# Causal mask of the row maxima: mask products on TensorE replaced by an add-and-max on VectorE

## The chip, the cores and the metric

One core of a Trainium2 chip runs the whole program. The metric is device time of the kernel in microseconds, the median of several runs. Lower is better. The five engines of a core (TensorE for matmul, VectorE, ScalarE, GpSimd, SyncE) each run their own instruction stream in program order and meet only at semaphores.

## What is computed

For each of 16 batches of 512 tokens with 256 features, a gated block of attention and a feed-forward net:

```python
xn = layernorm(x)
q, k, v = proj(Wq), proj(Wk), proj(Wv)          # 16 heads of 16
scores = einsum('bhsd,bhtd->bhst', q, k)
scores = where(triu(ones((S, S)), k=1), -inf, scores)
attn = softmax(scores / sqrt(D))
s = einsum('bhst,bhtd->bhsd', attn, v) @ Wo.T
g = silu((silu(xn @ wg.T) * (xn @ wu.T)) @ wd.T)   # wg, wu, wd: integers / 127
out = x + s * g
```

All is fp32. The kernel reaches fp32 accuracy by splitting most operands into a high and a low part (fp32r).

## The kernel before

The work of one batch is cut into units, each with a two-letter name and an index. Three hand-written tables (`HEAD`, `PERIOD`, `TAIL`) give the one order in which all engines walk through the units. `PERIOD` is run 13 times, and one pass of it is one batch's worth of work, with units of three neighbouring batches mixed (the second number of a unit says how many batches ahead it belongs). A unit function such as `u_sm` is called once for each engine, and emits that engine's part.

The units that matter here:

- `sm` (lines 419 to 437): scores of queries by keys, needed only for the maximum of each row. There are 22 such units in a batch, listed in `MAXIMA` (line 35). Query block `i` (0 to 3) needs the keys 0 to 128(i+1). A unit fills two banks of PSUM (one bank for the even head of each pair and one for the odd head) with as many pairs of heads as fit: 4 pairs at i=0 (2 x 4 x 128 columns), 2 at i=1 (2 x 2 x 256), 1 at i=2 (2 x 384) and 1 at i=3 (2 x 512). Over a batch that is 2 units with i=0, 4 with i=1, 8 with i=2, and 8 with i=3.
- `mk` (lines 439 to 457): TensorE adds the causal mask to the diagonal block of those scores by four small bf16 products a unit, and signals `f_sm`. VectorE waits for `f_sm`, takes the maxima of both banks in one `tensor_reduce` into `row_max`, and signals `d_sm`.
- `mt` transposes the maxima. Negated, they go by DMA into spare rows of `q_stack`, so that the products of the `st` units give score minus maximum, keys by queries. ScalarE takes their exponential, GpSimd zeroes what is above the diagonal, and `pv` multiplies by v.
- `gg`, `gu`, `hs`, `dn` are the feed-forward net. VectorE takes part in each (lines 366, 379, 416). `la` are the layer norm's statistics (lines 225 to 233).

PSUM has seven banks for all this (`RING`) and an eighth for `pv`. The last numbers of a unit in a table are its banks. Before TensorE writes a bank, `prev` waits for the release of the bank's last user; for `sm` that is `d_sm`, VectorE's maximum (line 42). A piece of `PERIOD` (lines 92 and 93):

```python
v 2 0 2, sm 2 6 34, mk 2 6 34, st 1 14 01, sm 2 7 56,
mk 2 7 56, pv 1 6, sm 2 8 34, mk 2 8 34, st 1 15 12, xr 1 0, sm 2 9 56
```

So `sm 8` on banks 3 and 4 can't start before the maximum of unit 6 on the same banks is taken.

At the start, GpSimd fills constants (lines 738 to 769), the mask's two factors `PICK` and `MASK` among them, and only then begins its part of the units, whose first is the power in line 237.

Of the kernel before, what the change touches and what calls it, by code (L numbers as in the profile page):

```python
# [4 lines left out]
FP32, F32R, BF16, INT32 = mybir.dt.float32, mybir.dt.float32r, mybir.dt.bfloat16, mybir.dt.int32  # L5
ACT = mybir.ActivationFunctionType
ALU = mybir.AluOpType
AX = mybir.AxisListType

P = 128  # L10
B, S, E = 16, 512, 256
# [5 lines left out]
TT = S // P  # L17
PAIRS = H // 2
HALF = 2 * P
STACK = 64  # L20
# [3 lines left out]
SCALE_S = 1.0 / D ** 0.5  # L24
EPS = 1e-5
MASKED = -3.0e38

COUNT = dict(
    f_gm=3, d_gm=3, f_tr=2, d_xm=1, f_qk=4, f_v=2, f_gg=FT, f_gu=FT, f_dn=2, f_op=2, f_mt=2, f_sm=22, f_st=20, f_pv=12,
# [79 lines left out]
def build(nc, x, xT, wqT, wkT, wvT, woT, wgT, wuT, wdT, out, scratch_o, scratch_r, scratch_m):  # L109
    with ExitStack() as ctx:  # L110
        def sb(name, shape, dt=FP32):
            return ctx.enter_context(nc.sbuf_tensor(name, shape, dt))

        def sem(name):
            return ctx.enter_context(nc.semaphore(name))
# [14 lines left out]
        QS = [sb(f"q_stack{i}", [P, PAIRS, S]) for i in range(2)]  # L130
        KS = [sb(f"k_stack{i}", [P, PAIRS, S]) for i in range(2)]
        V = [sb(f"v{i}", [P, TT, H, VW]) for i in range(2)]
        MX = sb("row_max", [P, 2, P])
# [16 lines left out]
        PICK = sb("mask_rows_bf16", [P, 2, P], BF16)  # L150
        MASK = sb("causal_mask", [P, 4, 64], BF16)
        ZERO = sb("zeros", [P, 512], BF16)

        PS = ctx.enter_context(nc.psum_tensor("bank", [P, RING, 512], FP32))
        PVB = ctx.enter_context(nc.psum_tensor("values", [P, 512], FP32))
# [1 line left out]
        sems = {name: sem(name) for name in COUNT}  # L157
        s_flag, s_lowrow, s_half = sem("s_flag"), sem("s_lowrow"), sem("s_half")
        s_first = [sem(f"s_first{t}") for t in range(TT)]
        s_const, s_fixed = sem("s_const"), sem("s_fixed")  # L160
        s_zeros, s_ones, s_kfill, s_qfill = sem("s_zeros"), sem("s_ones"), sem("s_kfill"), sem("s_qfill")
        s_w = {w: sem(f"s_w{w}") for w in W}
        c_wf, c_wh, c_wl = sem("c_wf"), sem("c_wh"), sem("c_wl")
# [6 lines left out]
        def r(ap):  # L170
            return ap.bitcast(F32R)

        def both(banks):
            return PS[:, banks[0]:banks[1] + 1:banks[1] - banks[0], :]
# [5 lines left out]
        def wait(e, s, value):  # L180

            if value > 0:
                e.wait_ge(s, value)

        def after(e, name, beta, k):
            wait(e, sems[name], nth(name, beta, k))

        def signal(ins, name):
            ins.then_inc(sems[name], 1)
# [229 lines left out]
        def u_sm(en, e, beta, par, k, banks, prev):  # L419
            i, pairs = MAXIMA[k]  # L420
            keys, half = P * (i + 1), k // (len(MAXIMA) // 2)
            if en == "pe":
                if k % (len(MAXIMA) // 2) == 0:
                    for which in range(2):
                        wait(e, s_stack[2 * half + which], 48 * (beta + 1))
                    if half == 0 and beta == 1:
                        e.wait_ge(s_rows, 32)
                    elif half == 0 and beta > 1:
                        wait(e, s_zero, 16 * (beta - 1))
                prev(e)  # L430
                for j, pair in enumerate(pairs):
                    for parity, n in enumerate(banks):
                        low = 64 * parity
                        nc.tensor.matmul(PS[:, n, j * keys:(j + 1) * keys],  # L434
                                         r(QS[par][low:low + STACK, pair, i * P:(i + 1) * P]),
                                         r(KS[par][low:low + STACK, pair, 0:keys]), start=j == 0, stop=False,
                                         skip_group_check=True)

        def u_mk(en, e, beta, par, k, banks, prev):
            i, pairs = MAXIMA[k]  # L440
            keys, n, half = P * (i + 1), len(pairs), k // (len(MAXIMA) // 2)
            if en == "pe":
                for right in range(2):
                    for parity, m in enumerate(banks):
                        low = 64 * parity
                        scores = PS[:, m, 0:n * keys].rearrange("p (n t) -> p n t", n=n)
                        last = nc.tensor.matmul(scores[:, :, i * P + 64 * right:i * P + 64 * right + 64], PICK[low:low + 64, right, :],  # L447
                                                MASK[low:low + 64, 0:n, :], start=False, stop=right == 1, skip_group_check=True)
                signal(last, "f_sm")
            elif en == "dve":  # L450
                after(e, "f_sm", beta, k)
                if beta == 0:
                    e.wait_ge(s_const, 19)
                at = pairs[0] % (PAIRS // 2)
                rows = MX[:, half, 32 * half:32 * half + 32].rearrange("p (b n i) -> p b n i", b=2, i=TT)[:, :, at:at + n, i]
                scores = both(banks)[:, :, 0:n * keys].rearrange("p b (n t) -> p b n t", n=n)
                signal(e.tensor_reduce(rows, scores, axis=AX.X, op=ALU.max), "d_sm")  # L457
# [189 lines left out]
        def u_rw(en, e, beta, par, k, banks, prev):  # L647
            if en == "sp":
# [4 lines left out]
                e.dma_start(QS[1][MROW:P:4, :, :].rearrange("p a (i s) -> p (a i) s", i=2),  # L653
                            ZERO[0:32, :].bitcast(FP32).rearrange("p (o s) -> p o s", o=1).to_broadcast([32, 2 * PAIRS, 256]))\
                 .then_inc(s_rows, 16)
# [62 lines left out]
        def run(en, e):  # L718
            users = {}
            step(en, e, 0, HEAD[:BRANCH], users)  # L720
            if en != "pe":
                later_steps(en, e, users)
                return

            e.wait_ge(s_flag, 3)
            exact = e.value_load(FLAG[0:1, 0:1], min_val=0, max_val=1)
            with e.If(exact):
                short[0] = True
                later_steps(en, e, dict(users))
            with e.Else():  # L730
                short[0] = False
                later_steps(en, e, dict(users))
# [3 lines left out]
        @block.gpsimd  # L736
        def _(e):
            e.memset(ZERO[:], 0.0).then_inc(s_zeros, 1)
            e.memset(RDEN[:], 1.0).then_inc(s_ones, 1)
            e.memset(IDF[:], 0.0).then_inc(s_const, 1)  # L740
            e.memset(PICK[:], 0.0).then_inc(s_const, 1)
            e.memset(MASK[:], 0.0).then_inc(s_const, 1)
            e.memset(MINUS_HALF[:], -0.5).then_inc(s_const, 1)
            e.wait_ge(s_const, 4)
            e.affine_select(out=IDF[:], in_=IDF[:], compare_op=ALU.not_equal, fill=1.0, base=0,
                            pattern=[[-1, P]], channel_multiplier=1).then_inc(s_const, 1)
            for low in (0, 64):
                e.wait_ge(s_const, 5 + low // 64 * 3)
                for side in range(2):
                    rows = PICK[:, side, 64 * side:64 * side + 63]  # L750
                    e.affine_select(out=rows, in_=rows, compare_op=ALU.not_equal, fill=1.0, base=-low,
                                    pattern=[[-1, 63]], channel_multiplier=1).then_inc(s_const, 1)
                all_masked = PICK[:, 1, 0:64]
                e.affine_select(out=all_masked, in_=all_masked, compare_op=ALU.not_equal, fill=1.0, base=-low - 63,
                                pattern=[[0, 64]], channel_multiplier=1).then_inc(s_const, 1)
            e.affine_select(out=MASK[:], in_=MASK[:], compare_op=ALU.is_ge, fill=MASKED, base=-64,
                            pattern=[[0, 4], [-1, 64]], channel_multiplier=1).then_inc(s_const, 1)
            e.wait_ge(s_const, 12)
            e.memset(MASK[0:64], 0.0).then_inc(s_const, 1)
            e.wait_ge(s_const, 13)  # L760
            e.affine_select(out=MASK[0:64], in_=MASK[0:64], compare_op=ALU.is_ge, fill=MASKED, base=0,
                            pattern=[[0, 4], [-1, 64]], channel_multiplier=1).then_inc(s_const, 1)
            for row in (63, 127):
                e.wait_ge(s_const, 14 + row // 127)
                e.affine_select(out=MASK[:], in_=MASK[:], compare_op=ALU.not_equal, fill=MASKED, base=-row,
                                pattern=[[0, 4], [0, 64]], channel_multiplier=1).then_inc(s_const, 1)
            for v in V:
                e.memset(v[:], 1.0).then_inc(s_const, 1)
            e.memset(MX[:], 0.0).then_inc(s_const, 1)
            run("pool", e)  # L770

        @block.sync
# [12 lines left out]
        def _(e):  # L785
            half = PAIRS // 2
            e.wait_ge(s_zeros, 1)
            zeros = ZERO[:].bitcast(FP32).rearrange("p (o s) -> p o s", o=1).to_broadcast([P, PAIRS, 256])
            for m in range(2):
# [14 lines left out]
        def _(e):  # L804
            e.wait_ge(s_const, 16)
            e.wait_ge(s_zeros, 1)
            nc.tensor.matmul(PVB[:], ZERO[:, 0:P], ZERO[:], start=True, stop=True).then_inc(s_fixed, 1)
            run("pe", e)
# [28 lines left out]
```

## Time and profile before

| what | us |
|---|---|
| median of 3 runs | 947.63 (947.14 to 948.02) |
| span of the profiled execution | 945.8 |
| TensorE busy in it | 914.8 |
| VectorE busy in it | 707.2 |
| ScalarE, GpSimd busy in it | 585.8, 495.1 |

The profiled execution has no total time of its own beyond its span, which runs from the first to the last instruction. The span lies 1.8 us under the median. Matmuls overlap in the pipeline, so a sum of their durations, and the busy time of TensorE, say little of what one of them costs. The chain of work that ended last, and the distances between starts, say it better. An engine that waits shows as idle time before an instruction, with the instruction that released it.

### The profile page before, as it was taken

How to read it: one execution, taken by the hardware profiler on the slowest of the kernel's cores; microseconds unless marked ns; L12 is line 12 of the kernel's file. 1: busy time of each engine (PE TensorE's matmuls, PEld its weight loads, DVE VectorE, ACT ScalarE, POOL GpSimd, SP SyncE). 2: the span in 40 equal slices, each digit the busy share in tenths (PEclk: the TensorE clock that was granted, in tenths of full speed). 3: DMA queues.
4: the chain of work that ended last, by engine and by line, in shares of the span. 5: the costliest groups of instructions: out<-in, count | busy, mean ns of one | idle time of the engine just before them, and what ended most of it. 6: DMA issues, size and time to landing. Idle time of an engine off the chain costs nothing.

```text
span 945.8 us, 22760 instructions
## 1 busy us (share of the span) xinstructions
PE 914.8 (97%) x9065; PEld 685.6 (72%) x9065; DVE 707.2 (75%) x950; ACT 585.8 (62%) x796; POOL 495.1 (52%) x681
## 2 busy tenths in 40 slices
PE   3999999999999999999999999999999999999995
PEld 2777767776868777686877868777786867768654
DVE  5985868778696887868788786877778697776823
ACT  5356664757576675756657575665757557575771
POOL 4253553736456464645636455473745547364553
PEclk9999999999999999999999999999999999999999
DMA  6704235353353534535343453534345253543323
GB/s 221 213 25 170 84 116 169 100 198 132 134 164 127 170 106 179 154 125 171 129 151 126 170 152 117 176 132 158 130 148 162 104 185 120 175 131 135 118 93 98
DMA packets 84507, 133.97 MB, mean 142 GB/s; under 512 B 13680, under 2 KB 34928, under 8 KB 84336
## 3 DMA queue, kind: packets, MB, share of 16 engines
q1 hardware_dynamic: 84400, 132.47, 41.8%
q8 instruction: 75, 1.23, 0.5%
q14 instruction: 32, 0.26, 0.1%
HBM read 53.22 MB, written 25.75 MB: 83 GB/s over the span
## 4 chain that ended last, share of the span: by engine, by line
PE 91%; DVE 2%; DMA 2%; POOL 2%; issue 1%; ACT 1%; SPq 0%; POOLq 0%; ACTq 0%; DVEq 0%
PE bank L194 48%; PE values L525 15%; PE bank L434 12%; PE bank L492 11%; PE bank L447 4%; DMA o_reciprocals<-scratch_r 1%; ACT probs L500 1%; DVE row_max L457 1%; PE bank L463 1%; POOL o_compact L566 1%; PE bank L668 0%; DMA scratch_r<-sum_reciprocals 0%; DVE x_in L259 0%; DVE xt_lo L279 0%; DMA sums<-scratch_o 0%
## 5 line engine op out<-in xcount | busy, mean ns | idle before, releaser
L457 DVE TENSOR_REDUCE row_max<-bank 128x2 f32<-128x768 f32 (+3 forms) x352 | 384.9, 1124 | 63.5 <-PE bank L447 60.3
L500 ACT ACTIVATE probs<-bank 128x1024 f32<-128x1024 f32 x320 | 320.4, 1026 | 122.2 <-PE bank L492 120.8
L507 POOL TENSOR_SCALAR_AFFINE_SELECT probs<-probs 128x256 f32<-128x256 f32 (+1 forms) x448 | 194.0, 450 | 275.1 <-ACT probs L500 274.1
L525 PE MATMUL values<-probs,v 128*17 128x512 f32 (+3 forms) x2048 | 166.2, 436 | 0.9 <-POOL probs L507 0.9
L393 POOL TENSOR_TENSOR h_lo<-gated,h_hi 128x512 fp32r<-128x512 f32 x96 | 124.6, 1298 | 74.8 <-ACT h_hi L390 72.7
L434 PE MATMUL bank<-k_stack,q_stack 64*128 64x128 f32 (+3 forms) x1024 | 155.3, 363 | 1.5 <-DVE row_max L457 1.2
L492 PE MATMUL bank<-q_stack,k_stack 64*128 64x512 f32 (+3 forms) x1024 | 142.2, 350 | 1.3 <-DVE row_max L457 0.7
L434 PEld LDWEIGHTS bank<-k_stack,q_stack 64*128 64x128 f32 x1024 | 83.1, 186 | 66.9 <-issue 30.4
L492 PEld LDWEIGHTS bank<-q_stack,k_stack 64*128 64x128 f32 x1024 | 82.9, 186 | 39.1 <-issue 17.3
L366 DVE SCALAR_TENSOR_TENSOR gated<-gated,bank 128x512 f32<-128x512 f32 x96 | 65.8, 685 | 55.4 <-ACT gated L363 55.4
L194 PE MATMUL bank<-xt_hi,wg_hi 128*128 128x256 f32 x384 | 99.3, 293 | 1.6 <-DVE gated L379 1.6
L194 PE MATMUL bank<-wd_hi,h_hi 128*128 128x256 f32 x384 | 93.7, 284 | 3.3 <-POOL h_lo L393 3.3
L194 PE MATMUL bank<-xt_hi,wu_hi 128*128 128x256 f32 x384 | 96.0, 286 | 0.0
L194 PE MATMUL bank<-xt_lo,wg_hi 128*128 128x256 f32 x384 | 94.0, 279 | 0.0
L194 PE MATMUL bank<-xt_lo,wu_hi 128*128 128x256 f32 x384 | 93.2, 279 | 0.0
L194 PE MATMUL bank<-wd_hi,h_lo 128*128 128x256 f32 x384 | 93.0, 282 | 0.0
L447 PE MATMUL bank<-causal_mask,mask_rows_bf 64*128 64x64 bf16 (+2 forms) x1408 | 84.6, 207 | 0.6 <-issue 0.6
L308 ACT ACTIVATE qk_hi<-bank 128x512 fp32r<-128x512 f32 x64 | 38.3, 598 | 74.6 <-PE bank L194 71.1
L525 PEld LDWEIGHTS values<-probs,v 128*17 128x17 f32 x2048 | 44.6, 96 | 47.6 <-issue 39.8
L194 PEld LDWEIGHTS bank<-xt_hi,wg_hi 128*128 128x128 f32 x384 | 73.3, 191 | 6.6 <-DVE gated L379 1.8
L194 PEld LDWEIGHTS bank<-wd_hi,h_hi 128*128 128x128 f32 x384 | 73.2, 191 | 4.5 <-POOL h_lo L393 3.5
L363 ACT ACTIVATE gated<-bank 128x512 f32<-128x512 f32 x96 | 57.6, 600 | 28.9 <-PE bank L194 28.4
(123 smaller groups left out, 1624.4 us busy)
## 6 DMA issues: line engine op xcount, KB each, us to landing
k_stack<-qk_hi SPq DMA_DIRECT2D x64, 256.0 KB, 2.5
q_stack<-qk_hi SPq DMA_DIRECT2D x64, 256.0 KB, 2.5
scratch_o<-o SPq DMA_DIRECT2D x64, 256.0 KB, 2.2
x_again<-x SPq DMA_DIRECT2D x16, 512.0 KB, 4.7
k_stack<-qk_lo SPq DMA_DIRECT2D x32, 256.0 KB, 2.5
q_stack<-qk_lo SPq DMA_DIRECT2D x32, 256.0 KB, 2.6
o_compact<-scratch_o SPq DMA_DIRECT2D x32, 256.0 KB
o_reciprocals<-scratch_r SPq DMA_DIRECT2D x32, 256.0 KB
```

Source lines behind the costliest of these rows:

```text
L194: last = nc.tensor.matmul(dst, r(lhs[a]), r(rhs[b]), start=start and j == 0, stop=stop and j == len(parts) - 1)
L308: signal(e.activation(r(QKP[0][:, k % 2, :]), PS[:, banks[0], :], ACT.Copy), "d_qh")
L363: signal(e.activation(T[:, slot, :], PS[:, banks[0], :], ACT.Tanh, scale=0.5 * SCALE_W), "d_t")
L366: signal(e.scalar_tensor_tensor(out=T[:, slot, :], in0=T[:, slot, :], scalar=1.0, in1=PS[:, banks[0], :], op0=ALU.add, op1=ALU.mult), "d_a")
L393: signal(e.tensor_tensor(r(HT[1][:, f:f + 2, :]).rearrange("p f s -> p (f s)"), T[:, slot, :], HT[0][:, f:f + 2, :].rearrange("p f s -> p ...
L434: nc.tensor.matmul(PS[:, n, j * keys:(j + 1) * keys], r(QS[par][low:low + STACK, pair, i * P:(i + 1) * P]), r(KS[par][low:low + STACK, pai ...
L447: last = nc.tensor.matmul(scores[:, :, i * P + 64 * right:i * P + 64 * right + 64], PICK[low:low + 64, right, :], MASK[low:low + 64, 0:n, ...
L457: signal(e.tensor_reduce(rows, scores, axis=AX.X, op=ALU.max), "d_sm")
L492: last = nc.tensor.matmul(PS[:, n, at:at + w], r(KS[par][low:low + STACK, pair, j * P:(j + 1) * P]), r(QS[par][low:low + STACK, pair, j * ...
L500: signal(e.activation(PR[:, (SCORES * beta + k) % SLOTS, :, :], both(banks), ACT.Exp, scale=SCALE_S), "d_ex")
L507: last = e.affine_select(out=diag, in_=diag, compare_op=ALU.is_ge, fill=0.0, base=0, pattern=[[0, many], [1, P]], channel_multiplier=-1)
L525: last = nc.tensor.matmul(PVB[32 * c:32 * c + VW, j * P:S], V[par][:, j, 4 * g + c, :], PR[:, (SCORES * beta + 5 * g + kind) % SLOTS, pari ...
```

## The change

The four mask products of each unit go. TensorE signals `f_sm` at the last score product. VectorE takes, for each head and query block, one `tensor_tensor_reduce`: it adds a mask `CAUSAL` (bf16, in SBUF: zeros, then a triangle of -3e38) to the scores, writes the sum back into the bank, and writes the maximum over the row into one column of `row_max` as second output. The part of `CAUSAL` taken is its last 128(i+1) columns. Only the last instruction of a unit signals `d_sm`. `MASKED_BY_VECTOR = 0` makes this hold for all query blocks. GpSimd makes `CAUSAL` behind the other constants. `PICK` and `MASK` are still made.

```diff
+MASKED_BY_VECTOR = 0
+        CAUSAL = sb("causal_rows", [P, S], BF16)
@@ u_sm, TensorE
+                by_vector = i >= MASKED_BY_VECTOR
                 for j, pair in enumerate(pairs):
                     for parity, n in enumerate(banks):
                         low = 64 * parity
-                        nc.tensor.matmul(PS[:, n, j * keys:(j + 1) * keys],
...
+                        last = nc.tensor.matmul(PS[:, n, j * keys:(j + 1) * keys],
...
+                if by_vector:
+                    signal(last, "f_sm")
@@ u_mk
-            if en == "pe":
+            by_vector = i >= MASKED_BY_VECTOR
+            if en == "pe" and not by_vector:
...
+                if by_vector:
+                    if beta == 0:
+                        e.wait_ge(s_causal, 2)
+                    for parity, m in enumerate(banks):
+                        for j in range(n):
+                            scores = PS[:, m, j * keys:(j + 1) * keys]
+                            col = 32 * half + 16 * parity + TT * (at + j) + i
+                            last = e.tensor_tensor_reduce(out=scores, in0=scores, in1=CAUSAL[:, S - keys:S], scale=1.0, scalar=MASKED,
+                                                          op0=ALU.add, op1=ALU.max, accum_out=MX[:, half, col:col + 1])
+                    signal(last, "d_sm")
+                    return
@@ GpSimd, constants
+            e.memset(CAUSAL[:], 0.0).then_inc(s_causal, 1)
+            e.wait_ge(s_causal, 1)
+            e.affine_select(out=CAUSAL[:, S - P:S], in_=CAUSAL[:, S - P:S], compare_op=ALU.is_ge, fill=MASKED, base=0,
+                            pattern=[[-1, P]], channel_multiplier=1).then_inc(s_causal, 1)
```

## Rows read from the trace of the kernel before

**Rows 1.** The page: busy time and share of the span by engine.
```profile
PE 914.8 (97%) x9065; PEld 685.6 (72%) x9065; DVE 707.2 (75%) x950; ACT 585.8 (62%) x796; POOL 495.1 (52%) x681
```

**Rows 2.** Busy us (instructions) in stretches: period, its two parts, head, end.
```profile
core 0: us, PE busy (x) PEld busy (x) DVE busy (x) ACT busy (x) POOL busy (x), PEclk, DMA share, GB/s
296.30:352.10 55.80, 55.80 (x563) 42.01 (x563) 43.67 (x59) 35.81 (x50) 30.64 (x41) 1.00 0.44 146
...
309.90:346.70 36.80, 36.80 (x406) 25.15 (x403) 33.74 (x43) 24.16 (x32) 21.19 (x31) 1.00 0.52 170
...
346.70:365.80 19.10, 19.10 (x166) 16.96 (x167) 9.98 (x16) 11.72 (x19) 9.50 (x12) 1.00 0.27 100
...
31.00:71.00 40.00, 37.67 (x355) 29.74 (x355) 35.52 (x50) 17.35 (x23) 16.82 (x17) 1.00 0.34 92
...
111.00:151.00 40.00, 39.67 (x373) 27.78 (x371) 26.54 (x32) 26.57 (x36) 21.42 (x30) 1.00 0.36 118
```

**Rows 3.** Timeline around 344 us: start, us, engine, line, what.
```profile
343.79 2.36 DVE L457 TENSOR_REDUCE row_max<-bank 128x2 f32<-128x1024 f32 x2
...
345.34 0.58 PEld L492 LDWEIGHTS bank<-q_stack,k_stack 64*128 64x128 f32 x8 [0.85 <-DVE row_max L457]
```

**Rows 4.** Chain that ended last, 296.3 to 352.1 us, by line.
```profile
by line: PE bank L194 53.1%; PE values L525 17.4%; PE bank L434 13.5%; PE bank L492 11.8%; PE bank L447 3.8%; PE bank L463 0.7%
```

**Rows 5.** Groups of instructions on VectorE: busy us, mean ns, idle before.
```profile
L457 DVE TENSOR_REDUCE row_max<-bank 128x2 f32<-128x1024 f32 x128 | 152.3, 1221 | 4.3 <-PE bank L447 2.1
L457 DVE TENSOR_REDUCE row_max<-bank 128x2 f32<-128x768 f32 x128 | 119.3, 953 | 18.9 <-PE bank L447 18.8
...
L366 DVE SCALAR_TENSOR_TENSOR gated<-gated,bank 128x512 f32<-128x512 f32 x96 | 65.8, 685 | 55.4 <-ACT gated L363 55.4
...
L605 DVE SCALAR_TENSOR_TENSOR gates<-bank,gates 128x256 f32<-128x256 f32 x1 | 0.4, 425 | 0.0
...
L230 DVE BATCH_NORM_AGGREGATE mv<-stats 128x2 f32<-128x6 f32 x64 | 6.1, 157 | 0.6
```

**Rows 6.** VectorE's timeline in the score stretch; xN rows merge N instructions.
```profile
309.96 2.36 DVE L457 TENSOR_REDUCE row_max<-bank 128x8 f32<-128x1024 f32 x2 [1.94 <-PE bank L447]
...
316.94 1.82 DVE L457 TENSOR_REDUCE row_max<-bank 128x2 f32<-128x768 f32 x2 [0.16 <-PE bank L447]
...
329.73 1.23 DVE L457 TENSOR_REDUCE row_max<-bank 128x4 f32<-128x1024 f32 x1 [0.81 <-PE bank L447]
...
332.90 1.39 DVE L225 BATCH_NORM_STATS2 stats<-x_in 128x6 f32<-128x256 f32 x4
334.33 0.38 DVE L230 BATCH_NORM_AGGREGATE mv<-stats 128x2 f32<-128x6 f32 x4
...
341.36 4.79 DVE L457 TENSOR_REDUCE row_max<-bank 128x2 f32<-128x1024 f32 x4
346.06 0.53 DVE L551 RECIPROCAL sum_reciprocals<-sums 64x64 f32<-64x64 f32 x1
348.46 0.69 DVE L366 SCALAR_TENSOR_TENSOR gated<-gated,bank 128x512 f32<-128x512 f32 x1 [1.86 <-ACT gated L363]
```

**Rows 7.** Two other pairs on VectorE, 300.7 us on.
```profile
300.69 0.69 DVE L311 TENSOR_TENSOR qk_lo<-bank,qk_hi 128x512 fp32r<-128x512 f32 x1 [0.57 <-ACT qk_hi L308]
...
301.30 0.68 DVE L379 SCALAR_TENSOR_TENSOR gated<-bank,gated 128x512 f32<-128x512 f32 x1
```

**Rows 8.** Who waited for whom, 309.9 to 346.7 us: us in total, times, longest.
```profile
DVE row_max L457 <- PE bank L447: 3.7, 6, 1.9
...
PEld bank L434 <- DVE row_max L457: 1.3, 2, 0.8
...
PEld bank L492 <- DVE row_max L457: 0.8, 1, 0.8
```

**Rows 9.** GpSimd's timeline at the start.
```profile
0.80 0.52 POOL L738 MEMSET zeros<- 128x512 bf16 x1 [0.29 <-POOLq L820]
1.26 0.52 POOL L739 MEMSET o_reciprocals<- 128x512 f32 x1
...
2.71 0.29 POOL L745 TENSOR_SCALAR_AFFINE_SELECT identity<-identity 128x128 f32<-128x128 f32 x1 [0.23 <-POOL minus_half L743]
```

**Rows 10.** Chain that ended last, at the start: start us, us, what.
```profile
8.88 0.25 POOL row_max L769
9.14 1.01 POOL mv L237
```

More of the change, by code:

```diff
@@ L159, in build @@
         s_first = [sem(f"s_first{t}") for t in range(TT)]
-        s_const, s_fixed = sem("s_const"), sem("s_fixed")
+        s_const, s_fixed, s_causal = sem("s_const"), sem("s_fixed"), sem("s_causal")
         s_zeros, s_ones, s_kfill, s_qfill = sem("s_zeros"), sem("s_ones"), sem("s_kfill"), sem("s_qfill")
@@ L433, in u_sm @@
                         low = 64 * parity
-                        nc.tensor.matmul(PS[:, n, j * keys:(j + 1) * keys],
-                                         r(QS[par][low:low + STACK, pair, i * P:(i + 1) * P]),
-                                         r(KS[par][low:low + STACK, pair, 0:keys]), start=j == 0, stop=False,
-                                         skip_group_check=True)
+                        last = nc.tensor.matmul(PS[:, n, j * keys:(j + 1) * keys],
+                                                r(QS[par][low:low + STACK, pair, i * P:(i + 1) * P]),
+                                                r(KS[par][low:low + STACK, pair, 0:keys]), start=j == 0, stop=by_vector,
+                                                skip_group_check=True)
+                if by_vector:
+                    signal(last, "f_sm")
         def u_mk(en, e, beta, par, k, banks, prev):
```

## The prediction

> **What bounds the kernel now.** I read the page's engine table first, then busy time by stretches of one period, then VectorE's timeline and the waits in the stretch that holds the maxima. TensorE is busy for 97% of the span, VectorE for 75% [rows 1]. Read alone, that says: take work off TensorE and pay with VectorE's free quarter. The stretches say otherwise. One period is 55.8 us. VectorE's work in it is uneven: from 309.9 to 346.7 us it is busy 33.7 of 36.8 us, and in the rest of the period 10.0 of 19.1 us [rows 2]. All 22 maxima of the period lie in the first part, and so do all the mask products.
>
> In that part TensorE already waits for VectorE's maxima, 2.1 us in three waits [rows 8]. The last is typical: the weight loads of the units `st 8` and `st 9` sit 0.85 us until a maximum is done [rows 3]. VectorE is idle for 36.8 - 33.7 = 3.1 us of it [rows 2]: nine short gaps with 2.65 us, and 0.4 us at the ends and in slivers. In 1.8 us of the gaps it waits for mask products: 3.7 us [rows 8] less the 1.94 before the first maximum, which begin before the part [rows 6]. So the score stretch runs at VectorE's pace, to within 2.65 us, and only the other part at TensorE's.
>
> **What goes.** In the chain that ended last, the mask products hold 3.8% of a period [rows 4], 2.1 us. That is their real price on TensorE, not their duration. It is 16 x 2.1 = 34 us for the whole kernel, the most that the change can give. But all of it lies in the stretch where TensorE has VectorE ahead of it. I count of it only that the first maximum of a period can start earlier by its own unit's four products, 0.2 us.
>
> **What is added, the main instructions.** Per batch there are 16 heads x 4 query blocks = 64 instructions, over 128, 256, 384 and 512 columns. The trace has no VectorE instruction that writes to a bank or has two outputs. The nearest by operands read one bank and one SBUF tensor: 685 ns for 512 columns, 425 for 256 [rows 5]. That is 1.02 to 1.04 ns per column and 150 ns on top. What counts in a full queue is the distance between starts. Two such instructions in a row start 0.61 us apart [rows 7], so 533 ns for the columns at 1.042 ns and some 75 on top. Four of the statistics (256 columns) take 1.39 us with 0.41 for the last, 0.33 apart [rows 6], or 60 on top. I take 73. A head then costs 1333 + 4 x 73 = 1625 ns, a batch 26.0 us.
>
> **What is taken from VectorE.** The reductions by distance between starts: 2.36 us for two of 1024 with 1.22 for the last gives 1.14; 4.79 for four gives 1.19; 1.82 for two of 768 gives 0.87 [rows 5, 6]. A batch has 6 x 1.14 + 8 x 0.87 + 8 x 1.19 = 23.3 us. So the columns are the same in number and only 64 starts in place of 22 cost more: 26.0 - 23.3 = +2.7 us a batch.
>
> **What is added, the second output.** The row maximum has to leave the engine as a [128, 1] column in another memory than the sum. If this takes an instruction or a step of its own, it comes 64 times a batch. Bounds: nothing, and the 157 ns of VectorE's shortest regular instruction [rows 5]. Four of these take 0.38 us, so they start (0.38 - 0.157) / 3 = 75 ns apart [rows 6]. I take 77 ns, because a tiny step in a full queue is nearest to that row: 64 x 77 = 4.9 us a batch, with 0 and 10.0 as the ends. Together with the main part VectorE gets +7.6 us a batch (2.7 to 12.7).
>
> The Trainium skill (VectorE: DVE Perf Modes, "Two Vector instructions with no wait between them") says that an operation which also writes out its accumulator is two instructions, the main one and a read of the accumulator. No row of this trace shows one. It gives no price; by it the lower end would drop out.
>
> **Where it lies.** All 7.6 us fall into the stretch that VectorE paces. Of this:
> - 0.2 us is the extra of the last unit, behind which TensorE doesn't wait at once, since the product that holds it next asks for the maximum before (unit 20, ends at about 345.0, product starts at 345.34 [rows 3]); that also leaves 0.33 us of lag for free;
> - of the 2.65 us of gaps I let 1.65 be filled. The gaps in which VectorE waited for scores shrink when it is late and the scores come earlier. Those behind ScalarE's tanh (0.4) and behind `v` (0.81 before unit 13 [rows 6], for which TensorE first needs 1.4 us of other products) close only partly; I leave 1.0;
> - 0.2 us for the earlier first maximum.
>
> The stretch grows by 7.6 - 0.2 - 0.33 - 1.65 - 0.2 = 5.2 us. Could the lag go on into VectorE's free time behind it (9.1 us [rows 2])? Not while TensorE waits: the ring lets it be two maxima ahead at most (`sm 8` asks for maximum 6), and its feed-forward products stand behind them in its queue. What TensorE loses there isn't won back, as the second part runs at TensorE's pace.
>
> How many times? 13 passes of `PERIOD`, and batch 0 in the head, where VectorE is busy 35.5 of 40 us [rows 2]. Batches 1 and 15 are looser (26.5 of 40 at 111 us [rows 2]), and I count them as one. 15 x 5.2 = 78 us.
>
> **At the start** GpSimd makes `CAUSAL` before its first unit. A fill of this shape takes 0.46 us from start to start, a wait and a select 0.23 + 0.29 less some overlap [rows 9]. These constants are on the chain right up to the power of line 237 [rows 10], so +0.9 us, in full.
>
> Sum against the profiled span: 945.8 + 78 + 0.9 = 1024.7 us. The median lies 1.8 above the span: 1026.5, so 1027.
>
> **Rivals.**
> - *No overlap (B).* The main instruction can't overlap what follows, since its maximum is read out behind it: 150 ns on top of the columns and 77 for the read-out; or equally the read-out takes the full 157. A head's main part is then 1333 + 600, a batch 30.9, so VectorE gets 7.6 + 4.9 = 12.5 us and the period 10.1: 15 x 10.1 + 0.9 = 152, which gives 1100 us. For it: no row of this trace shows a VectorE instruction with two outputs, so none excludes it. Against it: every chained pair here overlaps by about 75 ns. The Trainium skill (VectorE: DVE Perf Modes, "The DRAIN you can't avoid") says that the next operation doesn't start until the pipeline is empty, and would make this the rule. The trace disagrees for reductions, 1.14 us apart at 1.22 each.
> - *The read-out is free (C), the other side.* Then VectorE gets only 2.7 us. If TensorE, lighter by 2.1, is always ahead and all 2.65 of gaps fill, the period changes by 2.7 - 0.2 - 0.33 - 2.65 - 0.2 = -0.7 us: 15 x -0.7 + 0.9 = -9.6, so 938 us. It decides from a read-out under some 10 ns (0.7 / 64). For it: only that no row shows a price.
> - *The lag is absorbed in the second part (D).* VectorE's total of 43.7 + 7.6 = 51.3 is under TensorE's 55.8 - 2.1 = 53.7, and the period would be 53.7: 15 x -2.1 + 0.9 gives 917 us. Against it is the ring of banks and that TensorE waits for maxima already today [rows 8].
> - *The change takes nothing off TensorE's path.* That is contained in the forecast: there the 2.1 us turn into waiting.
>
> **How the numbers follow.** My forecast (all read-outs between 30 and 110 ns, gaps as said) 0.57; B and what lies between 0.24; C 0.08; D 0.04; between C and the forecast, so nearly no change or a small loss, 0.04; something worse than B 0.03. The forecast's own range is 990 to 1060 (read-out of 50 to 105 ns: 64 x 15 x 27 ns = 26 us either way; all gaps filled or none: 15 us down, 25 up). For 8 in 10 I go up to B and a little over it, and down to a read-out of about 20 ns: 975 to 1108. A measurement can tell some 0.2% of this kernel from no change. Faster by more than that: C and D, 0.12. Within: 0.03. Slower: 0.85.
>
> **What would show it.** In the profile after, VectorE should be busy about 707 + 16 x 7.6 = 829 us (if read-outs count as busy), above 90% in the score stretch, with the maxima's waits for score products nearly gone. TensorE's waits for VectorE's maxima should grow from 2.1 to about 7 us a period, its weight loads' waits above all. A period should be 61 us. The start distance of two main instructions of 512 columns should be some 0.69 us with the read-out between. The second part of the period should stay at about 19 us; if it shrinks, D is at work. I am wrong if the instruction's columns run at another rate than 1.04 ns (a bf16 tensor beside a bank, or writing a bank), which no row excludes, or if TensorE's clock falls when it waits more; it is 1.00 in all stretches now [rows 2].

## The result, and the profile after

The changed kernel takes 975.75 us (974.77 to 977.07), the kernel before on the same chip 947.38. The ratio is 1.031, with an interval of 1.029 to 1.032: slower by 28 us. The direction was forecast, the size was not: 1027 was too much by 51 us. The time lies just above the lower end of the range, 975, and the loss is only 36% of the forecast one.

The page of the changed kernel, its engines (to be set beside rows 1) and its chain:

```profile
span 975.3 us, 21643 instructions
...
PE 898.4 (92%) x7657; PEld 652.2 (67%) x7657; DVE 783.3 (80%) x2646; ACT 585.5 (60%) x796; POOL 499.3 (51%) x683
...
PE 58%; DVE 35%; issue 2%; DMA 2%; POOL 1%; ACT 1%; SPq 0%; POOLq 0%; ACTq 0%; DVEq 0%
PE bank L196 38%; DVE bank L468 25%; PE values L542 8%; PE bank L509 7%; DVE row_max L468 4%; PE bank L437 4%; DVE gates L632 2%; DMA o_reciprocals<-scratch_r 1%; DVE gated L381 1%; DVE sum_reciprocals L568 1%; DMA scratch_r<-sum_reciprocals 1%; ACT probs L517 0%; POOL o_compact L583 0%; DVE gated L368 0%; DVE o_lo L593 0%
```

VectorE, with 707 us busy before, has 783; the prediction said 829. A third of the chain that ended last now runs through it, where before 91% of it was TensorE. The groups of VectorE by form, in answer to rows 5 (busy us, mean ns, idle before):

```profile
L468 DVE CUSTOM_DVE_ANT_0 bank<-bank,causal_rows 128x512 f32<-128x512 f32 x256 | 168.3, 727 | 1.5 <-PE bank L437 1.5
L468 DVE DVE_READ_ACCUMULATOR2_ANT row_max<- 128x1 f32 x1024 | 141.4, 138 | 0.0
L468 DVE CUSTOM_DVE_ANT_0 bank<-bank,causal_rows 128x384 f32<-128x384 f32 x256 | 137.2, 587 | 4.0 <-PE bank L437 2.0
L468 DVE CUSTOM_DVE_ANT_0 bank<-bank,causal_rows 128x256 f32<-128x256 f32 x256 | 100.9, 454 | 8.7 <-PE bank L437 8.7
...
L468 DVE CUSTOM_DVE_ANT_0 bank<-bank,causal_rows 128x128 f32<-128x128 f32 x256 | 64.7, 320 | 23.3 <-PE bank L437 23.3
```

There are 1024 read-outs, one for each maximum, of 138 ns each. VectorE's timeline shows how they lie:

```profile
329.66 0.73 DVE L468 CUSTOM_DVE_ANT_0 bank<-bank,causal_rows 128x512 f32<-128x512 f32 x1
330.31 0.14 DVE L468 DVE_READ_ACCUMULATOR2_ANT row_max<- 128x1 f32 x1
330.31 0.73 DVE L468 CUSTOM_DVE_ANT_0 bank<-bank,causal_rows 128x512 f32<-128x512 f32 x1
330.96 0.14 DVE L468 DVE_READ_ACCUMULATOR2_ANT row_max<- 128x1 f32 x1
```

The read-out is recorded beside the start of the next main instruction, and the mains start 0.65 us apart. For 384, 256 and 128 columns the distance is 0.51, 0.38 and 0.25 us. So one main with its read-out costs the columns at 1.04 ns and about 117 ns on top, where the prediction had 73 + 77 = 150.

Twelve passes of `PERIOD` can be compared whole. They lie between two equal marks (a run of 74 feed-forward products on TensorE): first the kernel before, then the changed one, columns as in rows 2.

```profile
184.91:854.46 669.55, 669.17 (x6745) 503.92 (x6745) 517.44 (x697) 430.06 (x589) 365.36 (x492) 1.00 0.43 146
```
```profile
187.76:879.70 691.94, 655.15 (x5689) 476.96 (x5689) 575.76 (x1969) 429.34 (x589) 368.25 (x492) 1.00 0.41 141
```

A period went from 55.80 to 57.66 us, +1.87. VectorE's busy time in it went from 43.12 to 47.98, +4.86, and its idle time from 12.68 to 9.68. The span's 29.5 us are 2.9 ahead of the first mark, 22.4 in the twelve periods and 4.3 behind the last.

Where in the period does it go? Below, one period is cut at VectorE's first maximum and at the reciprocal that follows the last one, for the kernel before and then for the changed one:

```profile
309.96:346.06 36.10, 36.10 (x400) 24.45 (x396) 33.20 (x42) 23.46 (x32) 20.50 (x30) 1.00 0.53 173
346.06:365.75 19.69, 19.69 (x169) 17.55 (x169) 10.47 (x17) 12.34 (x19) 10.14 (x12) 1.00 0.27 98
```
```profile
316.61:355.16 38.55, 35.48 (x317) 22.82 (x316) 37.32 (x147) 23.95 (x32) 21.01 (x31) 1.00 0.49 162
355.16:374.19 19.03, 19.03 (x163) 16.89 (x164) 10.47 (x19) 11.87 (x19) 9.58 (x12) 1.00 0.27 100
```

Cut so, and averaged over the twelve periods of each trace, the score stretch grew from 36.1 to 38.6 us. VectorE's busy time in it grew by 4.85 us (32.6 to 37.5), and its idle time there fell by 2.4, from 3.5 to 1.1. The rest of the period shrank from 19.7 to 19.1 us, with VectorE busy for 10.5 in both. So all of the extra work lies in the score stretch, as forecast.

Who waited for whom, in the whole run (us, times, longest):

```profile
PEld bank L437 <- DVE row_max L468: 38.5, 54, 1.5
...
DVE bank L468 <- PE bank L437: 35.5, 36, 1.7
...
PEld bank L509 <- DVE row_max L468: 30.9, 49, 1.0
...
PE bank L509 <- DVE row_max L468: 14.8, 31, 0.7
...
PE bank L196 <- DVE row_max L468: 13.5, 14, 1.0
PE bank L437 <- DVE row_max L468: 12.3, 34, 1.3
```

The weight loads wait for maxima for 69 us in these two rows, 34 before. TensorE's matmul row itself, which showed 1.2 us of such waits before, has 41 us. In the twelve periods the weight loads' waits went from 2.1 to 4.6 us a period. VectorE's waits for scores, 60.3 us before, are down to 35.5.

### The profile page after: what moved, and what is told of

Read it like the earlier page. It is cut to its first block, busy times and chain, and to the rows that moved or that the text cites. A ratio compares the mean times of both kernels' runs of the same rounds, so it can differ in the third digit from the quotient of the medians.

```text
span 975.3 us, 21643 instructions
## 1 busy us (share of the span) xinstructions
PE 898.4 (92%) x7657; PEld 652.2 (67%) x7657; DVE 783.3 (80%) x2646; ACT 585.5 (60%) x796; POOL 499.3 (51%) x683
## 4 chain that ended last, share of the span: by engine, by line
PE 58%; DVE 35%; issue 2%; DMA 2%; POOL 1%; ACT 1%; SPq 0%; POOLq 0%; ACTq 0%; DVEq 0%
PE bank L196 38%; DVE bank L468 25%; PE values L542 8%; PE bank L509 7%; DVE row_max L468 4%; PE bank L437 4%; DVE gates L632 2%; DMA o_reciprocals<-scratch_r 1%; DVE gated L381 1%; DVE sum_reciprocals L568 1%; DMA scratch_r<-sum_reciprocals 1%; ACT probs L517 0%; POOL o_compact L583 0%; DVE gated L368 0%; DVE o_lo L593 0%
## 5 line engine op out<-in xcount | busy, mean ns | idle before, releaser
L468 DVE CUSTOM_DVE_ANT_0 bank<-bank,causal_rows 128x128 f32<-128x128 f32 (+3 forms) x1024 | 466.2, 522 | 37.6 <-PE bank L437 35.5
L524 POOL TENSOR_SCALAR_AFFINE_SELECT probs<-probs 128x256 f32<-128x256 f32 (+1 forms) x448 | 196.7, 456 | 292.1 <-ACT probs L517 291.1
L437 PE MATMUL bank<-k_stack,q_stack 64*128 64x128 f32 (+3 forms) x1024 | 152.0, 365 | 12.6 <-DVE row_max L468 12.3
L468 DVE DVE_READ_ACCUMULATOR2_ANT row_max<- 128x1 f32 x1024 | 141.4, 138 | 0.0
L437 PEld LDWEIGHTS bank<-k_stack,q_stack 64*128 64x128 f32 x1024 | 80.0, 185 | 88.9 <-DVE row_max L468 38.5
L509 PEld LDWEIGHTS bank<-q_stack,k_stack 64*128 64x128 f32 x1024 | 84.8, 185 | 67.7 <-DVE row_max L468 30.9
L196 PEld LDWEIGHTS bank<-xt_hi,wu_hi 128*128 128x128 f32 x384 | 72.8, 190 | 7.1 <-DVE gated L368 4.0
L365 ACT ACTIVATE gated<-bank 128x512 f32<-128x512 f32 x96 | 57.6, 600 | 31.9 <-PE bank L196 31.5
```

What stands on the lines that cost most here:

```text
L196: last = nc.tensor.matmul(dst, r(lhs[a]), r(rhs[b]), start=start and j == 0, stop=stop and j == len(parts) - 1)
L365: signal(e.activation(T[:, slot, :], PS[:, banks[0], :], ACT.Tanh, scale=0.5 * SCALE_W), "d_t")
L437: last = nc.tensor.matmul(PS[:, n, j * keys:(j + 1) * keys], r(QS[par][low:low + STACK, pair, i * P:(i + 1) * P]), r(KS[par][low:low + STA ...
L468: last = e.tensor_tensor_reduce(out=scores, in0=scores, in1=CAUSAL[:, S - keys:S], scale=1.0, scalar=MASKED, op0=ALU.add, op1=ALU.max, acc ...
L509: last = nc.tensor.matmul(PS[:, n, at:at + w], r(KS[par][low:low + STACK, pair, j * P:(j + 1) * P]), r(QS[par][low:low + STACK, pair, j * ...
L524: last = e.affine_select(out=diag, in_=diag, compare_op=ALU.is_ge, fill=0.0, base=0, pattern=[[0, many], [1, P]], channel_multiplier=-1)
```

## The experiments

The theory was: VectorE sets the pace of the score stretch, TensorE's relief is worth little there, and VectorE's extra time comes out at the end. Its rivals were that TensorE's relief counts in full and is merely outweighed, and that the price lies in something else than the read-out and the number of starts. The kernels can be put beside each other by a period (us; the twelve periods of the trace, divided by twelve):

| kernel | us | period | VectorE busy in it |
|---|---|---|---|
| before | 947.4 | 55.80 | 43.12 |
| no mask, one reduction a unit | 924.0 | 54.27 | 42.79 |
| no mask, wide units by head | 930.2 | 54.52 | 43.43 |
| no mask, narrow units by head | 936.5 | 55.01 | 43.98 |
| no mask, all by head | 944.2 | 55.54 | 45.01 |
| plain add in place, no maximum | 944.9 | 55.63 | 45.04 |
| add-and-max without read-out | 944.0 | 55.52 | 45.16 |
| changed | 975.8 | 57.66 | 47.98 |
| changed, and the products | 991.0 | 58.45 | 48.24 |

**The gain without the price.** From the changed kernel, VectorE's part of a unit back to one reduction, with no mask anywhere:

```diff
-                if by_vector:
+                if False:
                     if beta == 0:
                         e.wait_ge(s_causal, 2)
```

> No mask anywhere in the maxima: the mask products are gone, VectorE takes the maximum of each unit in one reduction as before, over all its columns, the masked ones too. It is an upper bound of the masked maximum, so the softmax is the same but for rounding; what is left out is the masking of the maxima, and with it the guard against a masked score that lies so far above all others of its row that the exponentials vanish. CAUSAL is still made. This is the gain of the change without its price. Theory (VectorE sets the pace of the score stretch): TensorE's 2.1 us a period become 1.2 to 1.7 us only, because VectorE's 2.65 us of gaps can't all close; 922 to 929 us. Rival (TensorE sets the pace all along): the whole 2.1 us times 16, 914 us. TensorE should wait for maxima more than the 2.1 us a period of before.

It took 923.99 us, ratio 0.975 (0.973 to 0.976). So taking the products off TensorE is worth 23.6 us (947.59 before, on the same chip), 1.53 us a period of the 2.1 that they hold in the chain, within what the theory said and clear of 914. The weight loads' waits for maxima grew to 3.0 us a period, as expected. The changed kernel lies 52 us above this one: that is the price of its work on VectorE, of which the relief of TensorE pays back 24.

**The products put back under the changed VectorE.**

```diff
-                if by_vector:
-                    signal(last, "f_sm")
...
-            if en == "pe" and not by_vector:
+            if en == "pe":
...
-            e.affine_select(out=CAUSAL[:, S - P:S], in_=CAUSAL[:, S - P:S], compare_op=ALU.is_ge, fill=MASKED, base=0,
+            e.affine_select(out=CAUSAL[:, S - P:S], in_=CAUSAL[:, S - P:S], compare_op=ALU.is_ge, fill=0.0, base=0,
```

> The changed kernel with the mask products put back on TensorE; VectorE still adds a row (now all zeros, since the products already mask) and takes the maximum. TensorE has the work of before, VectorE that of the changed kernel. Theory (VectorE sets the pace): the products fall mostly into TensorE's waits and cost 0.2 to 0.9 us a period: 979 to 990 us. Rival (TensorE's own work still counts in full): 975.8 + 33 = 1009 us.

991.01 us, ratio 1.046 (1.044 to 1.047), 15.3 us over the changed kernel. The period grew by 0.79 of the products' 2.1. The same products are worth 1.53 a period with 22 reductions and 0.79 with 64 add-and-max instructions. TensorE's work counts less the more VectorE holds it up. It doesn't count for nothing, as the time came out 1 us above the theory's range (979 to 990).

**The number of starts.** No mask, but 64 plain reductions a batch:

```diff
-                            last = e.tensor_tensor_reduce(out=scores, in0=scores, in1=CAUSAL[:, S - keys:S], scale=1.0, scalar=MASKED,
-                                                          op0=ALU.add, op1=ALU.max, accum_out=MX[:, half, col:col + 1])
+                            last = e.tensor_reduce(MX[:, half, col:col + 1], scores, axis=AX.X, op=ALU.max)
```

> No mask in the maxima (left out, as in the run without any mask), but VectorE takes them one head and query block at a time, 64 plain reductions a batch in place of 22: as many instructions as the changed kernel has, with no second output, no added row and nothing written to a bank. Theory (part of the price is the number of starts, the rest the read-out): starts 75 ns on top of the columns, so 0.61 us for 512 columns; VectorE gets 64 x 42 ns = 2.7 us a period less than in the changed kernel, and the time is 935 to 945 us. Rival (only the number of instructions counts): distances of 0.65 us as in the changed kernel, and 974 to 977 us.

944.21 us, ratio 0.996 (0.995 to 0.997). The groups of 512 columns of this run:

```profile
L468 DVE TENSOR_REDUCE row_max<-bank 128x1 f32<-128x512 f32 x256 | 156.4, 679 | 1.8 <-PE bank L437 1.6
```

156.4 us for 256 of them is 0.61 us each, and the four forms together take 26.6 us a batch. The 42 starts more than the unmasked kernel has cost 20 us; what the changed kernel adds on top of them costs 31.5 us.

**What makes the rest: the write into the bank, or the read-out?** First a plain add in place of the add-and-max, same operands, written back into the bank, no maximum:

```diff
+                            last = e.tensor_tensor(scores, scores, CAUSAL[:, S - keys:S], ALU.add)
```

> As the changed kernel, but each instruction is a plain add of the mask row, written back into the bank, with no maximum taken: the maxima are left out and stay zero. So two sources and a write to a bank, without the read-out. Theory (a write to a bank costs nothing of its own, the read-out about 40 ns): distances as for reductions of one head, 0.61 us for 512 columns, time within 3 us of that run. Rival (the write to the bank or the bf16 operand is what costs): 0.65 us and the changed kernel's 975 us.

944.85 us, ratio 0.997 (0.996 to 0.998). Then the very instruction of the change, but without its second output:

```diff
-                            last = e.tensor_tensor_reduce(out=scores, ...
+                            last = e._custom_dve(bass._DVE_TTR_OPS[(ALU.add, ALU.max)], out=scores, in0=scores, in1=CAUSAL[:, S - keys:S],
+                                                 s0=MASKED, s1=1.0)
```

> The changed kernel with the same add-and-max instruction, but its maximum is not written out, so there is no read-out; the maxima are left out and stay zero. Theory (the read-out is what lengthens the distance between starts, by 40 ns): 0.61 us for 512 columns, and 943 to 946 us, as in the run with plain adds. Rival (the add-and-max itself is slower than a plain add): 0.65 us and 974 to 977 us.

944.03 us, ratio 0.998 (0.997 to 0.998). The three agree within a microsecond, and so do their distances; the first row is of the plain add, the second of the add-and-max without read-out:

```profile
L468 DVE TENSOR_TENSOR bank<-bank,causal_rows 128x512 f32<-128x512 f32 x256 | 156.9, 690 | 1.7 <-PE bank L437 1.6
```
```profile
L468 DVE CUSTOM_DVE_ANT_0 bank<-bank,causal_rows 128x512 f32<-128x512 f32 x256 | 156.7, 688 | 1.8 <-PE bank L437 1.6
```

A second source, a bf16 operand, a write to the bank and the fused maximum cost nothing that these runs can tell beside a plain reduction of as many columns. The read-out alone takes the distance from 0.61 to 0.65 us and the time from 944.0 to 975.8: 1024 x 0.04 = 41 us of VectorE, of which 32 arrive at the end. In the table's terms, VectorE's busy time grows by 2.0 us a period from the kernel before to the one without read-out, and by 2.8 more with the read-outs.

**Does the place count?** The kernel before, with one useless reduction on VectorE in each batch. Once in the thick of the maxima:

```diff
                 signal(e.tensor_reduce(rows, scores, axis=AX.X, op=ALU.max), "d_sm")
+                if k == 8:
+                    e.tensor_reduce(PAD[:, 2 * beta:2 * beta + 2],
+                                    ZERO[:].rearrange("p (o s) -> p o s", o=1).to_broadcast([P, 2, 512]), axis=AX.X, op=ALU.max)
```

> The kernel before with one useless reduction of 1024 columns of zeros on VectorE in each batch (1.15 us), put behind the maximum of unit 8, in the middle of the score stretch. Theory (VectorE sets the pace there): 0.5 to 1.15 us a batch come out at the end, 955 to 966 us. Rival (what VectorE gets is taken up by its idle time wherever it lies): 947 to 949 us.

And once ahead of the first maximum, behind `gu`'s product of unit 1:

```diff
                                               in1=T[:, slot, :], op0=ALU.mult, op1=ALU.mult), "d_h")
+                if k == 1:
+                    e.tensor_reduce(PAD[:, 2 * beta:2 * beta + 2],
+                                    ZERO[:].rearrange("p (o s) -> p o s", o=1).to_broadcast([P, 2, 512]), axis=AX.X, op=ALU.max)
```

> The kernel before with the same useless reduction, but behind the product of the up projection's unit 1, where VectorE next waits 1.9 us for the first scores. Theory and its rival agree on no change, 946.5 to 949 us; a loss as large as in the dense stretch would mean that it isn't the place that counts but the total.

In both runs VectorE also waits once for the zeros, at the start. In the dense place the time is 962.85 us, ratio 1.017 (1.015 to 1.018): 16 us for 16 instructions, and a period of 56.66, +0.86. In the loose place it is 948.99, ratio 1.002 (1.001 to 1.003), with a period of 55.74, which is no longer than before. Its profiled span is 3.5 us longer than that of the kernel before: 2.7 more ahead of the first mark, 0.6 less in the twelve periods, 1.5 more behind the last. VectorE's timelines, first the dense place:

```profile
324.27 2.46 DVE L458 TENSOR_REDUCE row_max<-bank 128x2 f32<-128x1024 f32 x2
326.64 1.21 DVE L460 TENSOR_REDUCE pad<-zeros 128x2 f32<-128x1024 bf16 x1
327.77 2.35 DVE L458 TENSOR_REDUCE row_max<-bank 128x2 f32<-128x1024 f32 x2
```
```profile
310.92 1.21 DVE L383 TENSOR_REDUCE pad<-zeros 128x2 f32<-128x1024 bf16 x1
312.94 2.36 DVE L461 TENSOR_REDUCE row_max<-bank 128x8 f32<-128x1024 f32 x2 [0.81 <-PE bank L451]
```

In the first nothing is idle around it; in the second the wait of 1.94 us is down to 0.81 and the instruction has gone into it. VectorE is busy for 78 and 80% of a period in these two runs, so its total doesn't tell them apart.

**Which starts cost?** From the kernel with all maxima by head: first only the units of 384 and 512 columns by head (the others take the path of one reduction a unit), then, with `if i < 2`, only those of 128 and 256.

```diff
-                if by_vector:
+                if i >= 2:
```

> No mask in the maxima (left out, as in the run without any mask, 924.0 us). The units with 384 and 512 columns take them by head, 32 reductions in place of 16 a batch; the others in one reduction a unit. 16 starts more, 1.2 us of VectorE a batch. Taking all 64 by head cost 20 us over the run without any mask. Theory (what counts is the place: these units lie in the dense stretches, where the padded kernel lost 0.86 us a period for 1.13): 1.2 x 0.8 x 16 = 15 us more, 939 us. Rival (each start counts alike: 16 of 42): 8 us more, 932 us.

> The other half: only the units with 128 and 256 columns by head, 32 reductions in place of 6 a batch, 26 starts more, 2.0 us of VectorE a batch; no mask in the maxima. Theory (these units lie beside VectorE's waits, which take them up): 5 us more than the run without any mask, 929 us. Rival (each start counts alike: 26 of 42): 12.5 us more, 936.5 us.

930.19 and 936.51 us, ratios 0.982 (0.980 to 0.984) and 0.989 (0.987 to 0.992). The theory said 939 and 929, the rival 932 and 936.5. The rival is much the nearer. 6.2 us for 16 starts and 12.5 for 26 are 0.39 and 0.48 us a start. By the period the two differ more, +0.25 us and +0.74, or 16 and 28 ns a start, and it is the wide units, which lie closer together, that cost less. So the map of dense and loose stretches, which holds for one lump of 1.13 us, doesn't price small amounts spread over many units.

The periods also say how the parts add up: +0.25 and +0.74 alone, +1.27 together. The read-outs, put on top of that, cost 2.14 us a period. Against VectorE's busy time, the 42 starts cost 1.27 us for 2.2 more, the read-outs 2.14 for 2.8 more: 0.6 and 0.8 of what was added. Reckoned by distances, the starts come out cheaper still, 1.27 for 42 x 75 ns = 3.2 us, and the read-outs the same, 2.14 for 64 x 40 ns = 2.6. Whether the read-outs cost more for each microsecond because they come on top, or because of where they lie, no run separates.

**Only the widest block by VectorE.** The threshold at 3, `MASKED_BY_VECTOR = 3`:

> The changed kernel with the threshold at 3: only the last query block (512 columns, 8 units of a batch) is masked by VectorE, the other 14 units keep their products. VectorE gets 16 starts in place of 8, by distances 16 x 0.65 - 8 x 1.19 = +0.9 us a batch; TensorE loses 8 times 0.07 us. Theory (VectorE's extra counts by about 0.6): +0.9 x 0.6 less some 0.3 is +0.2 us a batch, 948 to 952 us. Rival (each masked block costs alike, 8 of 22 units of the change's 28 us): 958 us.

952.13 us, ratio 1.006 (1.004 to 1.008), just above the theory's range and clear of 958; the period is 56.06, +0.27. Even for this block alone (8 starts and 16 read-outs more in a batch, for 8 units' products less), the exchange loses.

**The start, and a faster kernel.** The threshold at 4 leaves only `CAUSAL` at the start; and the unmasked kernel without `CAUSAL`:

```diff
-            e.memset(CAUSAL[:], 0.0).then_inc(s_causal, 1)
-            e.wait_ge(s_causal, 1)
-            e.affine_select(out=CAUSAL[:, S - P:S], ...
```

> The changed kernel with the threshold at 4: no block is masked by VectorE, so it is the kernel before, but GpSimd makes CAUSAL at the start. Sum of the prediction: +0.9 us, 948.5. What the changed kernel's start showed: TensorE's first projection 0.4 us earlier than before, 947.0 to 947.5. The profile's start decides, as the times can't tell these apart well.

> As the run without any mask in the maxima (one reduction a unit), and CAUSAL isn't made at all: the version with the gain and none of the price; it leaves out the masking of the maxima. Theory (the start's constants hardly count, since the first instruction of the normalization is held by another thing at the same time): within 1.5 us of that run's 924.0. Rival (the constants count in full): 923 us, 0.9 less. A difference under 0.5 us can't be told.

948.80 us (1.0025, 1.001 to 1.004) and 922.68 us (0.975, 0.974 to 0.976). The first has a period of 55.81, as before, so its 2.4 us lie outside the periods. The second beats both kernels, by 24 us and 53 us, and by its ratio it can't be told from the unmasked one with `CAUSAL` (0.975 each). It gives up the masking of the maxima: with a masked score far above the others of its row the row's exponentials would vanish, and the two masking kernels are safe from that. The starts of these runs are told below.

## Why the prediction was right and wrong

**Half right: what bounds the stretch.** TensorE is 97% busy, and a trade at VectorE's cost still lost. The dense pad shows the pacing (+0.86 us for 1.13), the loose one the second part's free time, and the changed kernel's chain goes through VectorE for 35%. The sign to watch for, a second part that shrinks, came to 0.6 us a period, no more than the lag and the earlier first maximum in the forecast's own sum (0.33 + 0.2 + 0.2). But "the score stretch runs at VectorE's pace, to within 2.65 us" is too strong for the kernel before: with VectorE's load as it was, 1.53 of the 2.1 us taken off TensorE arrived. There the two engines wait for each other in turn, and work taken off or put on either of them comes out for some three quarters in these two runs (1.53 of 2.1, 0.86 of 1.13). Under the changed VectorE the same relief is worth 0.79 us a period, where the sum had 0.2 and what it let the earlier scores fill of the gaps.

**Right: the read-out exists.** "If this takes an instruction or a step of its own, it comes 64 times a batch": 1024 rows of it. The Trainium skill (VectorE: DVE Perf Modes, "Two Vector instructions with no wait between them") had said so, and the trace agrees: one row of a main and one of the accumulator read, 138 ns in each record of the latter.

**Wrong, and the step that failed: the price of the read-out.** The prediction set "I take 77 ns" on top of 73, +7.6 us a period. A read-out costs 40. A main and its read-out cost 117 ns on top together: by distance 16 x (0.25 + 0.38 + 0.51 + 0.65) = 28.6 us, where I had 26.0 + 4.9 = 30.9. The rows that the 77 was taken from are four short instructions in a row, 75 ns apart. The read-out is recorded beside the start of the next main, and lengthens the distance by 40 ns (0.61 to 0.65). The main part, 73 ns, held. With 40 in place of 77 the sum would have given 1027 - 64 x 15 x 37 ns = 991 us.

**Wrong: "VectorE gets +7.6 us a batch".** Its busy time grew by 4.86 a period: 2.0 for the main instructions, where the sum had 2.7, and 2.8 for the read-outs, where it had 4.9. The maxima's own rows grew by 5.6 (from 288.7 to 356.4 us over twelve periods). The other 0.8 are overlap: VectorE's other instructions are busy for 19.7 us a period in both traces, but more of their time lies under rows of the maxima, 1.5 us in place of 0.65. An instruction behind a wait shows its whole duration, and one behind another adds only its distance.

**Wrong in size: "of the 2.65 us of gaps I let 1.65 be filled".** By the cut at the first maximum and behind the last, VectorE's idle time in the score stretch fell by 2.4 us a period. In part this comes from which period was read: its stretch had 2.9 us idle, the mean of the twelve is 3.5. The lag behind the last maximum and the earlier first one were forecast at 0.73, and the rest of the period shrank by 0.62. Together: forecast 7.6 - 1.65 - 0.73 = 5.2, measured 4.85 - 2.37 - 0.62 = 1.86. Of the 3.3 us between them, 2.1 are the read-outs, 0.7 the main instructions and 0.7 the gaps, less 0.1.

**Wrong: the form of the sum.** It counts what is beyond the slack in full, and the runs show no such edge. From the unmasked kernel to that with all maxima by head to the changed one, the idle time in the stretch goes from 2.6 to 1.7 to 1.1 us, and of what VectorE gets 0.6 and then 0.8 arrive. A load that falls in small pieces over 22 units is partly taken up at every step, and the forecast by place, made for the two runs with part of the units by head, missed as well (939 and 929, measured 930 and 936.5). What the curve looks like between is open; only these points of it are measured.

**Right by luck: the count, and the lower end of the range.** 15 passes were close: 29.5 / 1.87 = 15.8. But 7.1 us of it lie outside the twelve periods, as much as 3.8 periods give, where the forecast took 3 by a guess, and no run says why the ends lost just that. The range reaches down to 975 for a read-out of 20 ns; the time came to lie at that end for other reasons.

**Rivals.** B (1100) fell: mains with read-outs do overlap what follows. By the rule of the Trainium skill on the drain (VectorE: DVE Perf Modes, "The DRAIN you can't avoid"), read as the prediction read it, 727 ns would be the distance, and the trace has 650. The same paragraph adds that a next operation that is not held starts earlier, and that fits. C (938) and D (917) fell as well. The run without read-out is C's condition: 944.0, a gain of 0.25%. So the sign of C was right and its 938 too low. By an estimate, if each ns of read-out costs the same 0.8 us (31.7 us for 40 ns), the change would break even at 3 to 4 ns, where C had "under some 10 ns".

**At the start** the sum had +0.9 us "in full". The power did end 0.9 us later, but the changed kernel's first projection started 0.36 us earlier than before. The constants alone (threshold 4) moved it 0.76 us later. The reason is below. The whole run with the constants alone is 2.4 us longer; of the 2.0 us in its profiled span 0.6 lie ahead of the first mark and 1.2 behind the last one, far from any constant. So no run shows the 0.9 as such at the end of the kernel.

## What to carry to other kernels

Read an engine's free time where the work will be put, not as a share of the span: here 25% free was 8% in the stretch, and it lost to take 2.1 us a period off TensorE and put 4.9 us on VectorE. Before splitting one instruction over many heads for the sake of a fused mask, count starts (75 ns) and read-outs (40 ns). Here the mask itself, the second source and the write-back were free; the 42 starts took 20 of the 24 us that the relief of TensorE gives, and the read-outs 32 more. And ask first whether the masked thing needs the mask: an upper bound of the row maximum gave the 24 us, at the price of the guard told above.

## What the hardware showed that was not expected

**A race at the start.** After GpSimd's power, VectorE has four normalizing instructions, and GpSimd casts weights that come by DMA. In the kernel before, a cast begins at 10.21, beside VectorE's first, and another at 12.21. VectorE's four take 3.76 us:

```profile
10.21 1.46 POOL L645 CAST probs<-probs 128x1536 f32<-128x1536 int32 x1
12.21 1.58 POOL L645 CAST probs<-probs 128x1536 f32<-128x1536 int32 x1 [0.54 <-DMA probs<-wuT]
```
```profile
10.17 3.76 DVE L259 TENSOR_SCALAR x_in<-x_in,mv 128x256 f32<-128x256 f32 x4 [4.57 <-POOL mv L237]
10.17 1.64 DVE L259 TENSOR_SCALAR x_in<-x_in,mv 128x256 f32<-128x256 f32 x1 [4.57 <-POOL mv L237]
12.38 1.55 DVE L259 TENSOR_SCALAR x_in<-x_in,mv 128x256 f32<-128x256 f32 x1
```

(The last two rows are the first and the fourth of the four.) In the changed kernel the power ends 0.9 us later, but the cast waits for its DMA, begins at 11.32 and meets only the second of the four:

```profile
11.05 2.53 DVE L261 TENSOR_SCALAR x_in<-x_in,mv 128x256 f32<-128x256 f32 x4 [5.54 <-POOL mv L239]
11.38 1.55 DVE L261 TENSOR_SCALAR x_in<-x_in,mv 128x256 f32<-128x256 f32 x1
```
```profile
11.32 1.46 POOL L662 CAST probs<-probs 128x1536 f32<-128x1536 int32 x1 [0.31 <-DMA probs<-wgT]
```

Over the traces of all runs, one of these instructions lasts 0.40 us by itself and 1.53 to 1.68 us beside a cast. In the kernel before that falls on two of the four, in the changed kernel on one. In the run with the constants alone the power is as late, but the casts come back to back from 10.97, ahead of VectorE at 11.05, and again meet two. TensorE's first projection starts at 18.13 there, against 17.37 before, 17.01 in the changed kernel and 16.10 in the last unmasked one. So a weight DMA that lands some tenths earlier or later decides over 1.1 us or so of the first projection.

It doesn't decide over the whole kernel. The two unmasked kernels differ only in `CAUSAL`; their first projections start 0.99 us apart (17.09 and 16.10), and their first marks lie at 179.17 and 179.22. Where the lead goes is open.

The Trainium skill (SBUF — State Buffer, "SBUF: two separate sides") says that VectorE in a two-port mode and GpSimd exclude each other from SBUF for a whole instruction. The rows agree in that the instruction that meets a cast ends 0.15 us behind it (11.38 + 1.55 = 12.93 against 11.32 + 1.46 = 12.78). That VectorE runs in such a mode here no row shows, and no run separates the two on purpose.

**TensorE's clock** stayed at 1.00 in all twelve periods, in spite of the 41 us for which its matmuls wait for maxima in the run: each of these waits lasted 1.3 us at most. The page's last slice of the changed kernel has 0.7, in the chain of DMAs at the end.
